# Products that nobody reads, issued to TensorE in waits, in a kernel of eight blocks on one core

## The reference

```python
x = x + L0_conv(ln_c(x))      # linear attention on qkv and on its 3x3 and 5x5 depthwise convolutions
t = t + L0_ffn(ln_t(t))       # mixture of 8 experts, the best two
x = x + L1_conv(ln_c(x))      # deformable convolution: offsets, bilinear gather of 36 samples, product
t = t + L1_ffn(ln_t(t))       # top half of the tokens by a router, gelu MLP
x = x + L2_conv(ln_c(x))      # four sigmoid gates and a scan: h = a*h + b*x; y = c*h + d*x
t = t + L2_ffn(ln_t(t))       # 8 experts of three products, mixed by a softmax over the batch mean
x = x + L3_conv(ln_c(x))      # depthwise 3x3, involution, depthwise 3x3
t = t + L3_ffn(ln_t(t))       # mixture of 8 experts, the best one, with a capacity
```

## Time and profile before

| | |
|---|---|
| Median of 3 runs | 633.27 us (632.72 to 633.65) |
| Profiled execution | 630.24 us |
| Its span, first to last instruction | 628.4 us |
| TensorE busy | 517.3 us (82%) |
| VectorE busy | 358.9 us (57%) |
| ScalarE busy | 283.9 us (45%) |
| GpSimd busy | 148.3 us (24%) |
| Mean granted TensorE clock | 0.947 of 2.4 GHz |

### The profile page before, as it was taken

One profiled execution on the slowest core, in us unless ns is written; L12 is line 12 of the kernel. 1 busy time (PEld: TensorE's weight loads), 2 busy tenths in 40 slices (PEclk: granted clock), 3 DMA queues, 4 the chain that ended last, 5 costly groups with the idle time before them and its releaser, 6 DMA issues. The chain is left out here.

```text
span 628.4 us, 12008 instructions
## 1 busy us (share of the span) xinstructions
PE 517.3 (82%) x5122; PEld 282.6 (45%) x5122; DVE 358.9 (57%) x574; ACT 283.9 (45%) x392; POOL 148.3 (24%) x140
## 2 busy tenths in 40 slices
PE   2889989968997994777787888757997898699994
PEld 0463338834223784766766642323323234333231
DVE  1253895165556437977886456465336696722534
ACT  2452222335551218999899526443671102333330
POOL 9900000020002000897887600006003002000000
PEclk9899999998999996999999897876999999799998
DMA  7000000020000005554453000110002000000000
GB/s 272 1 3 2 2 1 2 0 96 3 0 1 30 2 6 206 197 189 158 169 197 109 2 18 1 49 39 0 0 2 108 1 0 0 2 0 1 0 18 17
DMA packets 7989, 29.90 MB, mean 48 GB/s; under 512 B 864, under 2 KB 2176, under 8 KB 7552
## 3 DMA queue, kind: packets, MB, share of 16 engines
q1 hardware_dynamic: 7936, 29.14, 13.4%
HBM read 28.47 MB, written 0.67 MB: 46 GB/s over the span
## 5 line engine op out<-in xcount | busy, mean ns | idle before, releaser
L1008 PE MATMUL PS<-GX,OH 128*128 128x64 f16 x2304 | 74.5, 196 | 25.7 <-DVE OH L1170 19.3
L1008 PEld LDWEIGHTS PS<-GX,OH 128*128 128x128 f16 x2304 | 72.0, 100 | 30.3 <-DVE OH L1170 15.3
L1095 ACT ACTIVATE DIST<-BC,wbuf 128x2048 f16<-128x2048 f16 x24 | 48.0, 2001 | 2.6 <-DMA BC<-idx_dram 0.8
L1897 DVE TENSOR_SCALAR HID<-PS,wbuf 128x512 f32<-128x512 f32 x32 | 23.8, 750 | 41.6 <-PE PS L1790 41.6
L1098 ACT ACTIVATE OH<-DIST 128x2048 f16<-128x2048 f16 x24 | 45.9, 1911 | 0.8
L1170 DVE TENSOR_SCALAR OH<-BC,wbuf 128x2048 f16<-128x2048 f16 x48 | 44.1, 942 | 2.3 <-DMA BC<-idx_dram 2.3
L943 POOL TENSOR_TENSOR V<-SQ 128x512 f32<-128x512 f32 x18 | 27.9, 1550 | 58.7 <-DVE SQ L1181 57.9
L144 PE MATMUL PS<-X,wconst 128*128 128x512 f32 x32 | 20.2, 765 | 24.0 <-DMA wconst<-pack_dram 9.7
L1786 PE MATMUL PS<-Y,wbuf 64*128 64x512 f32 x128 | 36.6, 615 | 2.3 <-DVE HID L1897 1.5
L1836 ACT ACTIVATE HID<-PS,wbuf 128x512 f32<-128x512 f32 x32 | 22.0, 687 | 36.4 <-PE PS L1790 36.4
L163 ACT ACTIVATE SQ<-PS 128x512 f32<-128x512 f32 x16 | 9.6, 597 | 63.2 <-PE PS L144 63.2
(11 more groups left out here) (301 smaller groups left out, 950.3 us busy)
## 6 DMA issues: line engine op xcount, KB each, us to landing
BC<-idx_dram SPq DMA_DIRECT2D x36, 512.0 KB, 4.0
wbuf<-pack_dram SPq DMA_DIRECT2D x1, 2082.5 KB, 11.7
wbuf<-pack_dram SPq DMA_DIRECT2D x1, 1656.0 KB, 7.0
wbuf<-pack_dram SPq DMA_DIRECT2D x1, 1494.5 KB, 6.3
wbuf<-pack_dram SPq DMA_DIRECT2D x1, 820.0 KB, 13.2
wconst<-pack_dram SPq DMA_DIRECT2D x1, 759.5 KB, 7.3
wbuf<-pack_dram SPq DMA_DIRECT2D x1, 732.0 KB, 4.1
wbuf<-pack_dram SPq DMA_DIRECT2D x1, 602.5 KB, 3.7
```

The lines of the kernel that those rows point to most:

```text
L1008: mm = pe.matmul(o, OH[:, s % NOH, qh, t * P:(t + 1) * P], src, start=(qh == 0 and part == 0), stop=(qh == 1 and part == 1))
L1095: after_act(act, act.activation(DIST[:, :], BC[:, s % NBC, :], ACT.Abs, bias=wt("negq1")))
L1897: dve.tensor_scalar(HID[:, n % 8, :], bank(2 + n % 4), wt("b1_3", 2 * e + m, 1), 0.0, ALU.add, ALU.max).then_inc(hid_in_v, 1)
```

## The change

A helper issues k products on TensorE whose result nobody reads, into a bank that is free at that point. The operands are constants in SBUF. They wait for no semaphore and signal none. It is called at fifteen places; two of these are in the layer norm, which runs eight times, so 289 products are added (578 instructions with the weight loads). Nothing is removed. At one place two waits change places, so that the added products stand before the later one; at another, two waits are added. The diff, with the context lines cut:

```diff
+        def keep_busy(pe, n, k):
+            at = AT["ident"][1]
+            for _ in range(k):
+                pe.matmul(bank(n), wconst[:, at:at + 64].bitcast(BF16), wconst[:, at:at + 256].bitcast(BF16), start=True, stop=True)
         def ln_pe(pe, n):
             for h in range(2):
                 pe.matmul(bank(h), wt("center"), ...).then_inc(ln_centered, 1)
+            keep_busy(pe, 4, 4)
             for h in range(2):
                 pe.wait_ge(ln_squared, 2 * n + h + 1)
...
                 mm.then_inc(ln_var, 1)
+            keep_busy(pe, 4, 8)
             for h in range(2):
                 pe.wait_ge(ln_rstd, 2 * n + h + 1)
...
                 mm.then_inc(proj_ps, 1)                     # end of the first block
+                keep_busy(pe, 0, 10)
...
                     mm.then_inc(f0_ps, 1)                   # end of the second
+                keep_busy(pe, 5, 10)
...
+                pe.wait_ge(idxt_in, NB)                     # third, ahead of the gathers
+                keep_busy(pe, 6, 32)
                 pe.wait_ge(gx_done, 2 * NB)
-                pe.wait_ge(idxt_in, NB)
                 for s in range(SAMPLES):
                     gather(s)
...
                 project(4)                                  # end of the third
+                keep_busy(pe, 4, 10)
...
                                   start=(m == 0), stop=(m == 1)).then_inc(hid_used, 1)
+                    if n == 0:                              # fourth, after the first down projections
+                        keep_busy(pe, 4, 14)
...
                     mm.then_inc(wm_ps, 1)                   # end of the fourth
+                keep_busy(pe, 5, 16)
...
                         pe.matmul(bank(gbank[2 * k + h]), wt("ssw", k * P, P), ...).then_inc(gate_ps, 1)
+                pe.wait_ge(gate_in, 4)                      # fifth, during the scan
+                keep_busy(pe, gbank[0], 24)
+                pe.wait_ge(gate_in, 8)
+                keep_busy(pe, gbank[0], 24)
...
                 first(0)
                 first(1)
+                keep_busy(pe, 5, 10)                        # sixth
                 for n in range(0, BEFORE_WT, 2):
                     step(n)
...
                     pe.matmul(bank(h), wt("bo2"), rhs, start=False, stop=True).then_inc(f_ps, 1)
+                keep_busy(pe, 2, 10)                        # end of the sixth
...
                     mm.then_inc(o_ps, 1)
+                keep_busy(pe, 0, 10)                        # end of the seventh
...
                 mm.then_inc(g_ps, 1)
+                keep_busy(pe, 5, 18)                        # eighth, behind the router products
                 pe.wait_ge(oh_ready, 1)
...
                     mm.then_inc(t_ps, 1)
+                keep_busy(pe, 5, 5)                         # eighth, behind the transposes
                 pe.wait_ge(t_in, 4)
```

## The result

The changed kernel takes 639.77 us (median of 4 runs, 639.16 to 640.47), the kernel before 633.0 beside it (632.01 to 633.65): ratio 1.013, interval 1.010 to 1.017. The forecast was 640.8. The ratios in this document stand with their intervals as they are on record and aren't the quotient of the two medians, which is 1.011 here: by the medians the change costs 6.8 us, by the ratio 8.4 (6.2 to 10.6). In a later group of runs, on another chip, the same pair gave 638.44 and 630.15, ratio 1.013 (1.009 to 1.016).

What follows compares the result with a forecast made beforehand. A chain of eight blocks on one core, TensorE busiest, its clock mostly 2.4 GHz; added work costs what outlasts idle time. Costs +14.95, gains -7.4, net +7.5 us on 633.3 gives 640.8 us; range 635 to 646.

Steps and rivals of the forecast that it cites:

- The pace: Each added product of 512 bf16 columns takes 0.216 us of TensorE at 2.4 GHz.
- rival A: Added products stream faster, about 0.13 us each, so most fit into idle time: 626 to 629 us; chance 0.07.
- The scan: Fifth block: 48 products outlast 6.1 us of idle time; +4.3 us, or +4.6 with drain and barrier.
- The ends: Block ends: added products outlast VectorE's writing of X; five at +1.2 us (+0.96 to +1.43), the first +0.45.
- The layer norms: Seven layer norms at full clock: 12 added products each delay variances and spread, +0.6 us each (+0.4 to +1.0), +4.2.
- The covered places: Before the gathers (32), fourth block (14), last block (18 and 5): products lie inside waits and cost nothing.
- The two centrings: Centrings at 398 and 419 us, behind the fourth block and the scan, return to full clock: -3.1 us together.
- The fourth block: Its chain alternating between TensorE and ScalarE, slow from 384.72 us, ends 2.5 us sooner at full clock (0 to 3.1).
- rival C: More slow stretches vanish than counted, such as those near 47, 357 and 374 us: 637.3 to 639.8 us; chance 0.15.
- The sixth: Sixth block's start: first pair still slow, then ten added products partly bring the clock back; -0.8 us.
- The first layer norm: Its spread, at 1.2 GHz before, runs at 2.4 GHz behind eight added products: -1.0 us (0 to -1.7).
- B: The clock falls all the same and the gains are gone: 648 us, up to 652; chance 0.12.

Runs made afterwards that it cites:

- the doubled scan: Changed kernel with 48 and 48 added products in the scan instead of 24 and 24: 650.45 us, ratio 1.0306 to the kernel before.

## Why the prediction was right

**The pace** was right: 0.216 forecast, 0.2158 in the doubled scan. This decides the sign. At the pace of rival A the change would have been faster.

**The scan** was right: +4.3 forecast, +4.57 in the profile. The upper bound (drain and barrier) is what happens.

**The ends** were right in mechanism and low in size: 1.2 each forecast and 0.45 for the first, 1.53 three times, 1.43 twice and 0.78 measured, 8.2 us in all instead of 6.45. The open question was whether the barrier waits for TensorE to drain. It does: the centring starts 0.30 us after the modelled end of the last added product at all seven ends. The term should have been taken at its upper bound, 1.43, and even that was 0.1 short in blocks 2 to 4.

**The layer norms**: 0.6 forecast, 0.72 to 0.74 measured. The step that was short is the variance groups: I had them start 2.65 and 2.9 us after the first centring product, and the eight products 3.1 after it; they start at 2.75, 2.99 and 3.33. The spread starts at 5.06 instead of my 4.87. The bounds held it.

**The covered places** cost nothing that shows, as forecast: the wait of the up projections after the 14 is 0.3 us, the 18 of the last block end at 547.2, 0.5 us ahead of the count, and ahead of the gathers TensorE still waits 0.4 us for the first one-hot matrix.

**The clock's gains.** The two centrings: 1.67 and 1.40 less, net of the layer norm's 0.74, forecast 3.1 for both. The fourth block: -2.11 with an end of +1.53 in it, so 3.6 by the clock; forecast 2.5, because I took the stretch at 374 us as staying slow, and it went: there rival C was right. Whether the products did that isn't shown: of the eleven profiles with the 14, six have a stretch there. With it block 4 takes 22.8 to 23.3 us and without it 21.95, where no more than 9 products stand at the end. The sixth: -0.05 with +1.43 in it, 1.5 instead of 0.8, with the first pair of products at half clock as forecast (2.08 us). The first layer norm: -0.55 instead of -1.0, and that isn't shown to be the products' doing: without any in the layer norms it takes 9.64 to 11.10 us in the profiles, with the 12 9.74 to 10.92. The eighth: 0.5 gained at its start, and 1.7 lost to the slow stretch at 607 us, where I had 0; the changed kernel's other profile lacks that stretch. The gathers gave nothing that can be told from their variation, as forecast.

**The sum.** By the two profiles it is +10.2, and the forecast span of 635.9 us was 2.8 short; my costs were too small by 3 us (measured: 5.2 in layer norms, 8.2 at ends, 4.6 in the scan, 18.0 instead of 14.95), and my gains by the clock were about right in all, with single ones off both ways. By the medians it is +6.8 and, on the second chip, +8.3; the forecast of +7.5 lies between. That the total came so close is in part luck: the costs alone were off by 3 us, and single executions of one kernel differ by more than that. I had put what a measurement can tell at 1.3 us; the intervals here reach some 2 us to either side.

**The rivals.** A fell with the doubled scan. B (the clock falls all the same) fell in the windows at 385, 398 and 415. What I held against it was too strong, though: the clock isn't up in every busy stretch of the kernel before, for at 374.48 us TensorE is busy for 3.37 of 3.41 us at half clock. C holds in part: the slow stretches near 47 and 374 us went, but others came at 88, 317, 341 and 607 us, and not the same ones in the other profile.

What stays open: why the time of a single execution varies as it does, and with it what puts a slow stretch into one execution and not into the next. The kernel before had single times from 627.2 to 635.7 us in one group of runs. Block 1 behind its layer norm took 114.15 to 114.19 us in the six profiles without a slow stretch in it and with at most six products at its end, and 115.7 to 117.8 in the three with one or two such stretches and none at its end. Where they fall was not made to happen by any run.

## What to carry to other kernels

Work that nobody reads costs nothing in a wait and its full length behind one, so count it against the wait: the idle time before the next instruction that needs the engine, less the barrier's own 0.3 us and the drain. Sized that way the same idea turned 8 us of loss into 9 of gain here, on the same chip. Put it ahead of the stretches in which the next stage really waits for TensorE; 14 products in one wait brought 4.9 us, 32 in front of gathers that ScalarE paces brought nothing that could be measured.

## What was not expected of the hardware

- With the 14 products from 381.7 us the clock was in one execution still up at the centring 10 us behind their end, after 2.33 us of idle time; in another, with the same 14 and the same idle time, it was not.
- The slow stretches are not at the same places in two executions of one kernel: the changed kernel had one at 607 us in one profile, worth 1.7 us, and none in the other.
- Products of 64 columns, 1/8 of the columns at the same count, did not hold the clock at three places where those of 512 columns did.
- The barrier at a block's end waits for TensorE's last product, also for one that nobody reads and that signals nothing: 0.30 us lie between its modelled end and the next block's first product, at all seven ends.
